# Moving the second expert matmul, the mix and the order of exponents and scores in a one-core transformer layer pair

## What is computed

```python
x = x + attn_a(layernorm(x))   # 16 heads of 8, softmax over all keys, then a causal 0/1 mask on the weights
x = x + ffn(layernorm(x))      # router, top 2 of 8 experts and one shared expert, each (silu(x@w1) * (x@w3)) @ w2
x = x + attn_b(layernorm(x))   # 16 heads of 8 with rotary embedding, softmax, output projection and bias
x = x + ffn(layernorm(x))      # the same experts again
```

## Time and profile before

| What | us |
|---|---|
| median of 3 runs | 1905.57 |
| lowest and highest | 1901.0, 1913.17 |
| the profiled execution, its own time | 1906.13 |
| its span in the trace | 1904.1 |
| mean granted TensorE clock in it | 0.976 of full speed |

### The profile page before, as it was taken

One profiled execution on the slowest core, in us unless ns is written; L12 is line 12 of the kernel. 1 busy time (PEld: TensorE's weight loads), 2 busy tenths in 40 slices (PEclk: granted clock), 3 DMA queues, 4 the chain that ended last, 5 costly groups with the idle time before them and its releaser, 6 DMA issues.

```text
span 1904.1 us, 44343 instructions
## 1 busy us (share of the span) xinstructions
PE 1852.5 (97%) x16816; PEld 885.6 (47%) x16816; DVE 1566.8 (82%) x3083; ACT 1432.9 (75%) x2840; POOL 883.0 (46%) x1210
## 2 busy tenths in 40 slices
PE   6999999999999999999999999999999999999997
PEld 3444444444444444444444444444444444444446
DVE  4988998888888888988889888988888888788826
ACT  3388887777777777777788787778877877777782
POOL 6142333455655567555643434435334454544520
PEclk8599998999999999999999999999999999999999
DMA  7111110000100101001100101001100010000000
GB/s 254 35 68 68 58 42 3 1 28 27 52 2 35 35 24 47 2 35 35 35 35 2 51 25 62 2 2 52 40 19 8 2 30 29 24 2 8 7 2 12
DMA packets 39380, 61.91 MB, mean 33 GB/s; under 512 B 5632, under 2 KB 20608, under 8 KB 39040
## 3 DMA queue, kind: packets, MB, share of 16 engines
q1 hardware_dynamic: 39168, 59.08, 9.5%
HBM read 30.74 MB, written 27.26 MB: 30 GB/s over the span
## 4 chain that ended last, share of the span: by engine, by line
PE 86%; DVE 9%; ACT 2%; issue 2%; POOL 1%; DMA 0%; DVEq 0%; ACTq 0%; POOLq 0%
PE ps_sum L1212 28%; PE ps_banks L1178 20%; PE ps_banks L1232 11%; PE ps_banks L1153 9%; PE ps_banks L1253 8%; DVE negmax L940 5%; PE ps_banks L1124 2%; PE ps_banks L1167 2%; PE ps_banks L1131 1%; DVE xn L958 1%; PE ps_banks L1110 1%; PE ps_banks L1223 1%; ACT sums L810 1%; PE ps_banks L1138 1%; PE ps_banks L1160 1%
## 5 line engine op out<-in xcount | busy, mean ns | idle before, releaser
L940 DVE TENSOR_REDUCE negmax<-ps_banks 128x1 f32<-128x512 f32 x2048 | 1280.7, 680 | 196.0 <-PE ps_banks L1153 192.4
L803 ACT ACTIVATE probs<-ps_banks 128x512 f32<-128x512 f32 x2048 | 1085.7, 604 | 195.2 <-PE ps_banks L1178 182.5
L1153 PE MATMUL ps_banks<-kx,qx 24*128 24x512 f32 x2048 | 650.0, 507 | 7.4 <-DVE hid L991 3.6
L1178 PE MATMUL ps_banks<-qx,kx 26*128 26x512 f32 x2048 | 528.6, 500 | 3.5 <-DVE hid L991 1.8
L1212 PE MATMUL ps_sum<-probs,vg 128*9 128x256 f32 (+1 forms) x6144 | 463.8, 374 | 6.8 <-ACT sums L810 6.0
L1178 PEld LDWEIGHTS ps_banks<-qx,kx 26*128 26x128 f32 x2048 | 197.3, 183 | 374.1 <-issue 168.1
L692 POOL TENSOR_SCALAR scaled<-scaled,gates 128x128 f32<-128x128 f32 x516 | 182.9, 372 | 283.1 <-ACT scaled L854 244.2
L1153 PEld LDWEIGHTS ps_banks<-kx,qx 24*128 24x128 f32 x2048 | 260.4, 185 | 103.6 <-ACT probs L803 55.1
L664 POOL TENSOR_TENSOR pdiag<-probs,causal 128x512 f32<-128x512 f32 x128 | 163.5, 1278 | 173.3 <-ACT probs L803 172.4
L680 POOL TENSOR_TENSOR hid<-hid,first 128x512 f32<-128x512 f32 x129 | 164.9, 1278 | 125.8 <-DVE hid L991 121.4
L1212 PE MATMUL ps_sum<-probs,w 128*9 128x256 f32 (+1 forms) x2560 | 187.7, 365 | 2.0 <-ACT sums L810 1.3
(11 more groups left out here) (104 smaller groups left out, 1289.0 us busy)
## 6 DMA issues: line engine op xcount, KB each, us to landing
qk_rows<-limbs SPq DMA_DIRECT2D x36, 512.0 KB, 3.5
qx<-qk_rows SPq DMA_DIRECT2D x128, 96.0 KB
kx<-qk_rows SPq DMA_DIRECT2D x128, 96.0 KB
qx<-mlimbs SPq DMA_DIRECT2D x512, 2.0 KB
qk_rows<-prod_c SPq DMA_DIRECT2D x8, 512.0 KB, 3.7
qk_rows<-prod_s SPq DMA_DIRECT2D x4, 512.0 KB, 2.7
out_dram<-x SPq DMA_DIRECT2D x8, 256.0 KB, 2.3
x<-in_x SPq DMA_DIRECT2D x3, 512.0 KB, 5.9
```

The lines of the kernel that those rows point to most:

```text
L803: act.activation(m.probs[:, blk % PROB_SLOTS, EXP_HEADS[k], :], bank, ACT.Exp, scale=SCALE).then_inc(s.freed[SCALAR], 1)
L940: dve.tensor_reduce(m.negmax[:, unit // UNITS % 2, half, col:col + 1], bank, AX.X, ALU.max, negate=True).then_inc(s.freed[VECTOR], 1)
L1153: pe.matmul(bank_of(("scores", unit, k)), m.qx[rows, n % SLOTS, tile * P:(tile + 1) * P], m.kx[rows, n % SLOTS, half * CHUNK:(half + 1) * ...
L1178: pe.matmul(bank, m.kx[rows, n % SLOTS, j * P:(j + 1) * P], m.qx[rows, n % SLOTS, half * CHUNK:(half + 1) * CHUNK], start=True, stop=True) ...
```

## The change

Three things change, in the planner alone; no instruction gets another operand.

1. In `feed_forward` h3 stands 1 step behind h1 (3 before), hidden 2 (4), the mix 11 (7) and the gate 13 (9). At the distance of 7 the mix of unit `k` therefore falls on step 4 of unit `k+1`, where it fell on step 0 of unit `k+1`, next to that unit's h1. At the distance of 5 it falls on step 1 of unit `k+2`, ahead of that unit's h3, where it stood alone on step 2 of unit `k+1`.
2. A step emits exp, score, exp, score where it emitted exp, exp, score, score. The copy of a span's sum comes behind the step's last weigh in the plan; it stood between the step's two exponents, so ACT now does one exponent more before it.
3. `LEAD` is 26 steps (30). Four units of scores leave the stretch before the loop and enter its end. The turned maximum of a span is due 7 steps before its first exponent (11).

The number of units in the loop stays 129: the last starts at step 1010, and 1010 + 13 is below 1024.

```diff
-LEAD = 30
+LEAD = 26
 TURN_AT = 2
 X_SLOTS = 3
+H3_AT, Y_AT, GATE_AT = 1, 11, 13
...
-    return staged(at, (0, ("h1", k)), (3, ("h3", k)), (4, ("hidden", k)), (7, ("y", k)), (9, ("gate", k)))
+    return staged(at, (0, ("h1", k)), (H3_AT, ("h3", k)), (H3_AT + 1, ("hidden", k)),
+                  (Y_AT, ("y", k)), (GATE_AT, ("gate", k)))
...
-            if free + 9 >= TOTAL:
+            if free + GATE_AT >= TOTAL:
...
         items += side.get(step, [])
+        both = scores_of(step + LEAD) if step + LEAD < TOTAL else []
         for k in range(2):
             items.append(("exp", blk, part * 2 + k))
-            whole = blk + 1 - WEIGH_LAG
-            if part and not k and whole > 0 and whole % NT == 0:
-                items.append(("copy", whole // NT - 1))
-        if step + LEAD < TOTAL:
-            items += scores_of(step + LEAD)
+            items += both[k:k + 1]
+        items += both[2:]
         if part and diagonal(blk):
             items.append(("mask", blk))
         if blk >= WEIGH_LAG:
             items.append(("weigh", blk - WEIGH_LAG, part))
+            if part and (blk + 1 - WEIGH_LAG) % NT == 0:
+                items.append(("copy", (blk + 1 - WEIGH_LAG) // NT - 1))
```

## The result

The changed kernel takes 1888.7 us (median; 1872.2 to 1902.0), the kernel before, measured beside it, 1905.95 us. The ratio is 0.990 with a 95% interval of 0.987 to 0.993: about 1% faster, where 2.4% was forecast. Each median is of twelve executions; the slowest one of the changed kernel (1902.0 us) lies over 1.5% above its fastest and is not in the ratio. The profiled execution took 1888.6 us with a span of 1886.7 us. Its mean granted TensorE clock is 0.960, where it was 0.976.

What follows compares the result with a forecast made beforehand. No single engine bounds the kernel: seven banks couple nearly equally loaded PE, DVE and ACT. 1906 - 40 (distance 7) - 22 (distance 5) + 20 (copy) - 4 (lead) = 1860 us, 2.4% faster; range 1800 to 1915 us.

Steps and rivals of the forecast that it cites:

- the forecast's own case: Whole kernel: the stalls at h1 go and the rest is as costed; 1860 us, range 1825 to 1885, chance 0.58.
- the value of 0 for alternation: Order exp, score in each step: at most 14 us gained where DVE bounds, set against rival C; taken as 0.
- C: Each step's second exponent, held behind a score needing a bank DVE frees, starves ACT; slower, 1926 us, chance 0.10.
- The mix away from h1, distance 7: 90 units: the 0.74 us stall behind h1 goes; 0.45 us per unit, 40 us gained, bounds 0 to 86.
- The clean unit: One undisturbed unit of 7 steps on PE's timeline: 10.71 us before, walked out to 10.25, a gain of 0.45.
- ACT would no longer idle ahead of the mix: Sign of a right forecast: ACT's idle time ahead of the mix, 0.76 us before, disappears.
- A switch each way: Pulling the mix from h1 adds a tiling-mode switch each way, agreeing with 0.19 us extra for a lone mix.
- The mix beside h3, distance 5: 36 units: a 0.73 us stall gives way to small ones of 0.4 us; 0.6 us per unit, 22 us gained.
- The copy: Copy one exponent later delays the weigh behind it by 0.53 us in 4/7 of 64 spans; +20 us, bounds 0 to +34.
- Lead 26: Four fewer units of scores before the loop save 4.6 us, the end costs slightly; -4 us in all.
- rival D: First exponents of many spans wait some us for a late maximum; slower, up to 1924 us, chance 0.05.
- Rival B: Half the saving at h1 reappears behind the lone mix and the copy costs its full 34 us; 1905 us, chance 0.17.

Runs made afterwards that it cites:

- the whole change with the old dealing: Changed kernel, late copy and alternating issue included, with only the banks dealt in the order exp, exp, score, score: 1860.1 us, ratio 0.975.
- the zero matmuls: Changed kernel plus four matmuls adding zero to the weighed sum in 27 further steps, each one step behind a normalisation: 1879.0 us, ratio 0.984.

## Why the prediction was wrong, point by point

**The sign and the wide range were right, the size was not.** 1860 us was forecast and 1889 came, which is also outside the 1825 to 1885 of the forecast's own case. Three terms of the sum were off. For the units and the lead it had -66 us, and offsets and lead together gave 2.5%, some -47. For the copy it had +20, and 3 to 8 came. So offsets and lead alone should have taken 1840 us by the sum, and took 1861. In the whole change with the old dealing the two errors nearly cancel, and it is by luck that it took 1860.1 us, the forecast's number. The step that leaves the gap of 29 us is the value of 0 for alternation.

**Alternation: taken as 0, measured 21 us with the offsets.** The rival that the prediction set against it (C: an exponent held behind a score on PE) is wrong as a mechanism, since with that issue order and the old banks the kernel takes 1857 us. The order rule cited there was not shown to cost anything. Of C only the remark on banks that DVE frees points the right way, and it was made for the exponents. What I missed stands in the code: the ring deals by order, so changing the order changes who frees the bank of each burst. I checked the partners of exponents and scores, and not those of h1 and the mix over the whole plan.

**No term for a change of the granted clock.** The sum took the time at half the clock as it was. In the profiled executions it is 2 x (1 - 0.960) x 1886.7 = 151 us after, against 2 x (1 - 0.981) x 1855.5 = 71 us in the kernel with offsets and lead. The first pair of windows above gives a price: 10.2 us lost in 29.36 us at 0.54, of which 2 x 0.46 x 29.36 = 27 us at half the clock, 0.38 us each. The second pair gives 0.43, and the changed kernel's own executions 0.40. 80 us times 0.40 is 32 us, and the spans differ by 31.2. That the clock follows PE's idleness is shown by the zero matmuls, which fill the same wait in the first stretch and keep the clock at 1.00 there.

**The mix away from h1, distance 7: 40 us forecast.** Offsets and lead give 1144.1 - 1118.6 = 25.5 us there, the whole change 6.5. The clean unit gained 0.23 us and not 0.45. The reason given, that ACT is late because of the mix, was wrong: the wait of 0.74 us is there without the mix in front. By the partners in the plan it comes from h1's own two passes on ACT, which precede the exponents whose banks the scores need, and h3 covers it when it stands in its place; that reading fits the traces and was not tested by itself. That ACT would no longer idle ahead of the mix was wrong too; in the changed kernel's clean unit it still does:

```profile
568.14 0.60 ACT L856 ACTIVATE scaled<-ps_banks 128x512 f32<-128x512 f32 x1 [0.69 <-PE ps_banks L1255]
```

The added cost of a lone mix was right to the row: 1.09 us, 0.19 more than with h1 behind it. The prediction set the Trainium skill's rule that a change of the tiling mode drains TensorE (TensorEngine Tiling, Key Properties) beside it. That page gives no time for it, and no run here tells the drain from another cause. "A switch each way" was also too many: with or without the mix, a weigh with 128 rows stands between the row-tiled matmuls of two steps.

**The mix beside h3, distance 5: 22 us forecast**, 17.2 measured with offsets and lead, 15.4 in the whole change. This step held, and its own figures (0.73 - 0.4 + 0.19 = 0.52 us per unit, where it wrote 0.6) give 19 us, nearer still.

**The copy: +20 us forecast**, +11 alone, and 3 to 8 in company, of which the calculation above leaves nothing but the clock. PE's waits for the copy, before and after, in the view of waits (us in total, times, longest):

```profile
PE ps_sum L1212 <- ACT sums L810: 7.3, 26, 0.4
```

```profile
PE ps_sum L1214 <- ACT sums L812: 20.7, 41, 0.8
```

The wait grew by 13 us and not by 20. The longest grew from 0.4 to 0.8 us, near the 0.53 of the forecast, but a third of the spans do not wait at all.

**Lead 26: -4 us forecast**, -10 alone, but between offsets without it (1862.9, ratio 0.979) and with it (1861.0, ratio 0.975) the intervals overlap: 2 us by the medians, 7 by the ratios. The maximum was never late: one wait of 0.4 us of PE's weight loads for these transfers is all that the changed kernel's view of waits lists, so rival D falls.

**Rival B** put the total at 1905 us, 16 us above what was measured, and for a reason that was not the right one: the gain of the units was not eaten at the lone mix, but in a few stretches at half the clock.

## What to carry to other kernels

Where buffers are dealt round a ring in program order, an exchange of two small items changes whose buffer every later large one waits for. List these partners from the plan before and after, for each kind of large item, and look in the trace at what each does when the engine that frees its buffer runs long work of its own: here h1 and the mix stood idle behind DVE, while the fastest kernels have h3 on DVE's banks in 108 of 129 units. Read the granted clock by stretch before trusting a sum of durations: here two waits of 1.35 and 1.19 us were followed by a slow stretch of 30 us that cost 10. If executions of one kernel differ in mean clock, the slope of time over half-clock time is its price, with no further run. Of the kernels run, the alternating issue with the old dealing and the old copy has the lowest median, 1857.3 us; offsets and lead (1861.0) and the whole change with the old dealing (1860.1) are the same within the noise, and all three are faster than before and after.

## What the runs showed of the hardware

The cost of idleness of PE was not local. With alternation two waits of 1.35 and 1.19 us, which ended at 957.07 and 963.87, were followed by 30.7 us at 1.2 GHz, in which DVE and ACT waited for PE. The windows of that kernel, all engines' busy time, ahead of the fall and behind it:

```profile
955.00:966.20 11.20, 8.58 (x76) 4.08 (x74) 11.20 (x20) 7.53 (x15) 4.49 (x7) 1.00 0.00 0
966.20:980.00 13.80, 13.80 (x76) 8.45 (x75) 5.70 (x11) 6.29 (x14) 2.50 (x2) 0.50 0.01 1
980.00:996.90 16.90, 16.90 (x98) 6.22 (x98) 10.47 (x21) 9.33 (x19) 4.66 (x8) 0.50 0.01 2
```

Ahead of it DVE was busy for the whole 11.20 us and PE for 8.58; behind it PE is busy throughout and DVE for 5.70 of 13.80 us. PE was the bound in that stretch although DVE had caused it. Nor did the fall come in the gap itself: PE had been busy again since 963.87, at 2.4 GHz, when the clock went down at 966.2. And alternating issue by itself does no harm: in the changed kernel the exponents and scores of a step on the four row groups start at 561.79 to 561.80, within 0.01 us as before. Each us at the lower clock cost 0.40 us here; it would be 0.5 if PE at half its speed had set the time in all of it.
